# A transformer block on one Trainium2 core: a new written-out order for the first eight slots, and small moves in quad 3 and at the end

## The reference, cut to what matters

```python
q = (x @ Wk.T + bk);  k = (ctx @ Wk.T + bk);  v = (ctx @ Wv.T + bv)      # per head, q and k share Wk
scores = einsum(q, k) / sqrt(32)                                          # causal
p = softmax(where(allow, scores, -1e32))
dist = sqrt(clip((sum(p) - cumsum(p)) * abs(i - j), 0))
effect = clip(exp(-softplus(gamma) * dist), 1e-5, 1e5)
attn = softmax(where(allow, scores * effect, -1e32))
x1 = layer_norm(x + concat(attn @ v) @ Wo.T + bo)
out = layer_norm(x1 + relu(x1 @ W1.T + b1) @ W2.T + b2)                   # 2048 hidden features
```

## Time and profile before

| | |
|---|---|
| median of 3 runs | 1573.59 us (1573.33 to 1576.73) |
| the profiled execution | 1576.78 us, its span 1575.0 us |
| PE, PEld, DVE, ACT, POOL busy | 1476.0, 1232.7, 1165.7, 1037.4, 102.6 us |
| granted PE clock, mean | 0.972 |
| DMA | 334.13 MB, mean 212 GB/s |

### The profile page before, as it was taken

The page is one execution under the profiler, slowest core; times in us unless marked ns, Lnnn a source line. Parts: engine busy times, 40 slices in busy tenths (PEclk is TensorE's granted clock), DMA queues, the critical chain, the costliest instruction groups (busy, mean ns, idle before and its releaser), DMA issues.

```text
span 1575.0 us, 34730 instructions
## 1 busy us (share of the span) xinstructions
PE 1476.0 (94%) x13056; PEld 1232.7 (78%) x13056; DVE 1165.7 (74%) x3971; ACT 1037.4 (66%) x2679; POOL 102.6 (7%) x97
## 2 busy tenths in 40 slices
PE   4567899999999999999999999999999999999897
PEld 3455788878878887887888788788878878888786
DVE  5787769687787968778696877869687786968533
ACT  2776766766667676666767666676766667676622
POOL 4000101000010100001010000101000010100000
PEclk8777999999999999999999999999999999999999
DMA  5774556555665655565555556656555665654776
GB/s 214 245 250 186 191 186 213 206 197 201 213 221 197 220 202 194 203 213 219 198 221 204 191 203 218 220 191 226 201 189 207 216 222 190 223 201 176 269 290 255
DMA packets 62790, 334.13 MB, mean 212 GB/s; under 512 B 8224, under 2 KB 8224, under 8 KB 29472
## 3 DMA queue, kind: packets, MB, share of 16 engines
q1 hardware_dynamic: 62624, 331.92, 58.6%
HBM read 306.72 MB, written 25.17 MB: 211 GB/s over the span
## 4 chain that ended last, share of the span: by engine, by line
PE 64%; DVE 26%; ACT 7%; issue 1%; DMA 1%; POOL 1%; SPq 0%; POOLq 0%; DVEq 0%; ACTq 0%
PE bank L205 18%; PE bank L207 16%; PE bank L206 16%; PE bank L401 7%; DVE w_sb L1028 6%; DVE w_sb L1016 5%; PE bank L415 4%; DVE gz L1024 2%; DVE w_sb L1038 2%; DVE s_sb L1004 1%; ACT w_sb L698 1%; ACT w_sb L700 1%; PE bank L437 1%; ACT w_sb L696 1%; DVE rows L1098 1%
## 5 line engine op out<-in xcount | busy, mean ns | idle before, releaser
L205 PE MATMUL bank<-xt_hi,w_ring 128*128 128x256 f32 x1024 | 296.0, 289 | 0.9 <-ACT h_sb L777 0.9
L207 PE MATMUL bank<-xt_hi,w_ring 128*128 128x256 f32 x1024 | 287.7, 281 | 0.0
L206 PE MATMUL bank<-xt_lo,w_ring 128*128 128x256 f32 x1024 | 287.2, 281 | 0.0
L719 ACT COPY pt_sb<-bank 128x512 f32<-128x512 f32 x192 | 111.8, 582 | 203.7 <-PE bank L415 203.6
L1004 DVE CUSTOM_DVE_ANT_0 s_sb<-bank,mask 128x256 f32<-128x256 f32 (+7 forms) x512 | 129.9, 303 | 155.4 <-PE bank L401 154.4
L205 PE MATMUL bank<-w_ring,h_hi 128*128 128x512 f32 x512 | 211.3, 413 | 7.9 <-DVE h_lo L1111 6.4
L689 ACT ACTIVATE w_sb<-s_sb,nm 128x161 f32<-128x161 f32 (+7 forms) x512 | 164.1, 404 | 77.7 <-DVE nm L1012 77.7
L709 ACT ACTIVATE p_sb<-w_sb,nm 128x32 f32<-128x32 f32 (+7 forms) x512 | 205.7, 405 | 0.0
L207 PE MATMUL bank<-w_ring,h_lo 128*128 128x512 f32 x512 | 203.9, 398 | 0.0
L206 PE MATMUL bank<-w_ring,h_hi 128*128 128x512 f32 x512 | 202.5, 396 | 0.0
L401 PE MATMUL bank<-qk_sb 32*32 32x256 f32 (+7 forms) x4096 | 170.5, 294 | 33.6 <-DVE m L1004 27.1
(11 more groups left out here) (130 smaller groups left out, 2989.5 us busy)
## 6 DMA issues: line engine op xcount, KB each, us to landing
w_ring<-w_split SPq DMA_DIRECT2D x256, 1024.0 KB, 4.8
w_split<-w_ring SPq DMA_DIRECT2D x32, 512.0 KB, 5.1
x_raw<-x_t SPq DMA_DIRECT2D x16, 512.0 KB, 3.9
c_raw<-ctx_t SPq DMA_DIRECT2D x16, 512.0 KB, 5.0
u_sb<-x_rows SPq DMA_DIRECT2D x16, 512.0 KB, 5.9
ring_raw<-w SPq DMA_DIRECT2D x32, 256.0 KB, 5.6
out<-rows SPq DMA_DIRECT2D x15, 512.0 KB, 6.9
wk_raw<-wk SPq DMA_DIRECT2D x1, 1024.0 KB, 4.8
```

The lines of the kernel that those rows point to most:

```text
L205: nc.tensor.matmul(dst, a_hi, b_hi, start=start, stop=False)
L206: nc.tensor.matmul(dst, a_hi, b_lo, start=False, stop=False)
L207: return nc.tensor.matmul(dst, a_lo, b_hi, start=False, stop=stop)
L719: nc.scalar.copy(pt_sb[:, n], pt_bank[:]).then_inc(pt_ok, 1)
```

## The change

- The first eight slots have an order of their own (`first`) on every engine, in place of `step(0)` and `step(1)`. In it DVE masks all three groups of a slot before `decayed_scores` of the slot before; the splits are spread 0, 3, 3, 2, 2, 4, 2, 0 over slots 0 to 7; the rows' stage of batch 0 is written out in slot (1, 2).
- The cast of each `w1`/`w2` piece moves from ACT to POOL. The pieces are split in the order 4 to 15, 0 to 3, and 0 to 3 stay in the ring: the first two pairs of batch 0 are not read back.
- `wk` is loaded, cast and subtracted in two parts: the 128 columns of quad 0 first, the rest after. `gammas` are loaded by ACT's queue with a semaphore of their own (`gam_in`), as is `bk` (`bk_in`). POOL makes its constants in another order, and DVE, ACT and PE wait for the part each needs (`MASKS`, `STARTS`, `DISTS`, `CONSTS`); the 16 column memsets are four with strides. `l1b_bc` and `add_bias(0)` move to slot 4 on POOL. `values(0, *)` and `values(1, *)` go to the y banks, in slots (0, 1), (1, 0), (1, 1).
- In `step`, quad 3, the masks of groups 0 and 1 come before `rows_low(i-1, 0)` and `concat_low(i, 0)`.
- At the end `hidden_low(14, 1)` moves from `final` to the end of `step(15)`; both `project_rows(15, *)` follow each other into two banks; `turn_rows(15, *)`, `hidden(15, 0)` are each moved ahead of an `add_hidden` of batch 14.

In the diff, calls that follow each other are put on one line.

```diff
-            for i in range(B):
-                step(i, True, 1 <= i, 2 <= i, 3 <= i, i + 1 < B)
+            first()
+            for i in range(2, B):
+                step(i, True, True, True, 3 <= i, i + 1 < B)
...
+        SPLIT = [*range(4, FT), *range(4)]
+        SPLIT_BY = (0, 3, 6, 8, 10, 14, 16, 16)
...                                                  # SP, per slot n of the first eight
+                    for at in split_in(n):
+                        store_hidden(at)
+                        if 1 <= at and at + 3 < FT:
+                            raw_hidden(at + 3)
...                                                  # PE, slots 0, 1 and 6
+                scores(0, 0, 0); scores(0, 0, 1); scores(0, 0, 2)
+                pe.wait_ge(qk_ok, 1)
+                pe.wait_ge(wk_lo_ok, 2)
+                queries_keys(0, 1)
+                scores(0, 1, 0); scores(0, 1, 1); scores(0, 1, 2)
+                pe.wait_ge(qk_ok, 2)
+                queries_keys(0, 2)
+                values(0, 0, y_bank[0])
+                values(0, 1, y_bank[1])
...
+                scores(1, 2, 0); scores(1, 2, 1)
+                transposes(1, 0, 0)
+                scores(1, 2, 2)
+                project_rows(0, 0)
+                project_rows(0, 1, y_bank[1])
+                transposes(1, 0, 1)
+                pe.wait_ge(u_ok, 1)
+                queries_keys(1, 3)
...                                                  # PE, end
                 project_rows(last, 0)
+                pe.wait_ge(pt_ok, 12 * B)
+                project_rows(last, 1, pt_bank)
+                add_hidden(ffn, 5)
+                hidden(ffn, 7)
                 pe.wait_ge(u_ok, RT * last + 1)
-                add_hidden(ffn, 5)
-                project_rows(last, 1)
-                hidden(ffn, 7)
-                add_hidden(ffn, 6)
-                pe.wait_ge(u_ok, RT * last + 2)
                 turn_rows(last, 0)
                 turn_rows(last, 1)
+                add_hidden(ffn, 6)
+                hidden(last, 0)
                 add_hidden(ffn, 7)
-                hidden(last, 0)
                 hidden(last, 1)
...                                                  # DVE, slots 2, 3 and 6
+                totals(0, 0); masks(0, 2); decayed_scores(0, 1)
+                running_sums(0, 2); splits(2)
+                totals(0, 1); masks(0, 3); concat(0, 0); decayed_scores(0, 2)
+                inputs_low(1); concat_low(0, 0); running_sums(0, 3); splits(3)
...
+                totals(1, 0); masks(1, 2); splits(5)
+                residual(0, 0); residual(0, 1, y_bank[1])
+                moments1(0); weigh1(0); shift1(0)
+                decayed_scores(1, 1); rows_low(0, 0); rows_low(0, 1)
+                running_sums(1, 2); splits(6)
...                                                  # DVE, step, quad 3
                     totals(i, 1)
-                if last:
-                    rows_low(i - 1, 0)
-                if now:
-                    concat_low(i, 0)
                     mask_scores(i, 3, 0)
                     mask_scores(i, 3, 1)
+                if last:
+                    rows_low(i - 1, 0)
+                if now:
+                    concat_low(i, 0)
...                                                  # POOL
+            def split_high(at):
+                n = SPLIT[at] % 4
+                pool.wait_ge(raw_in[n], 32 * (at // 4 + 1))
+                nc.gpsimd.tensor_copy(w_ring[:, n::4, 0], ring_raw[:, n::4, 1]).then_inc(ffw_hi_ok, 1)
```

More of the change, by code:

```diff
@@ L337, in step @@
                             w2_behind(i - 1, 0)
[L338 to L347, removed]
             def final():
                 step(B, False, True, True, True, False)
-            over_batches(step, final)
+            over_batches(first, step, final)
             rows_out(B - 2)
@@ L1136, in finish_rows, with splits, masks, first @@
                                                    ALU.mult, ALU.add).then_inc(out_ok, 1)
+            def splits(n):
+                for at in split_in(n):
+                    split_low(at)
+            def masks(i, c):
+                for g in range(NS):
+                    mask_scores(i, c, g)
+            def first():
+                masks(0, 0)
+                key_weight_low(1, slice(P, D))
+                dve.wait_ge(const_ok, DISTS)
+                running_sums(0, 0)
+                splits(0)
+                masks(0, 1)
+                weight_low(1, wv_lo, wv_hi, wv_raw)
+                decayed_scores(0, 0)
+                running_sums(0, 1)
+                splits(1)
+                totals(0, 0)
+                masks(0, 2)
+                decayed_scores(0, 1)
+                running_sums(0, 2)
+                splits(2)
+                totals(0, 1)
+                masks(0, 3)
+                concat(0, 0)
+                decayed_scores(0, 2)
+                inputs_low(1)
+                concat_low(0, 0)
+                running_sums(0, 3)
+                splits(3)
+                totals(0, 2)
+                masks(1, 0)
+                concat(0, 1)
+                decayed_scores(0, 3)
+                concat_low(0, 1)
+                weight_low(2, wo_lo, wo_hi, wo_raw)
+                running_sums(1, 0)
+                splits(4)
+                totals(0, 3)
+                masks(1, 1)
+                concat(0, 2)
+                decayed_scores(1, 0)
+                concat_low(0, 2)
+                running_sums(1, 1)
+                concat(0, 3)
+                concat_low(0, 3)
+                totals(1, 0)
+                masks(1, 2)
+                splits(5)
+                residual(0, 0)
+                residual(0, 1, y_bank[1])
+                moments1(0)
+                weigh1(0)
+                shift1(0)
+                decayed_scores(1, 1)
+                rows_low(0, 0)
+                rows_low(0, 1)
+                running_sums(1, 2)
+                splits(6)
+                totals(1, 1)
+                mask_scores(1, 3, 0)
+                mask_scores(1, 3, 1)
+                inputs_low(2)
+                hidden_low(0, 0)
+                concat(1, 0)
+                mask_scores(1, 3, 2)
+                decayed_scores(1, 2)
+                concat_low(1, 0)
+                running_sums(1, 3)
+                concat(1, 1)
+                concat_low(1, 1)
@@ L1343, in add_bias, with first @@
                                         ALU.add).then_inc(xb_ok, 1)
+            def first():
+                for at in range(4):
+                    split_high(at)
+                for n in range(2 * NQ):
+                    if n == 2:
+                        inputs_high(1)
+                    for at in split_in(n):
+                        if 1 <= at and at + 3 < FT:
+                            split_high(at + 3)
+                    if n == 4:
+                        pool.wait_ge(s_mm, NS * (NQ + 1))
+                        pool.wait_ge(cons_in, 16 * 6)
+                        pool.wait_ge(const_ok, CONSTS + 1)
+                        nc.gpsimd.tensor_tensor(l1b_bc[:], l1b_bc[:], b2_bc, ALU.add).then_inc(col_ok, 1)
+                        add_bias(0)
+                    if n == 6:
+                        inputs_high(2)
+                    if n == 7:
+                        add_bias(1)
             def step(i, now, last, ffn, done, ahead):
-                if i == 0:
-                    add_bias(0)
                 if ahead:
@@ L1354, in final @@
                 pass
-            over_batches(step, final)
-CONSTS = 4 + 6 + 1 + 16 + 1 + 12 + 1 + 1 + 1
-COLS = 8
+            over_batches(first, step, final)
+MASKS = 8 + 4
+STARTS = MASKS + 4
+DISTS = STARTS + 4 + 1
+CONSTS = DISTS + 8 + 1 + 1
+COLS = 3
 def kernel(**inputs):
```

344 lines of the change are left out of this document (252 added, 92 removed).

## The result

The kernel after takes 1564.68 us (median of 6 runs, 1564.31 to 1568.86), the kernel before 1575.10 in the same session (6 runs, 1573.33 to 1576.73): ratio 0.9937, interval 0.9927 to 0.9948. It gains 10.4 us where 21.7 were forecast. The sign is right and the time lies in the range, but the likeliest case had its own range of 1546 to 1558, and the time is outside it. The profiled execution (1566.3 us, span 1564.5) is 10.5 us shorter in span than that of before.

The account below looks back on a forecast made before the run. PE was taken to bound from batch 2 on, DVE's sum the first eight slots; 16.4 + 0.3 + 5.0 = 21.7 us off the 1573.59 us median gave 1552 us, range 1536 to 1565, likeliest case (0.50) 1546 to 1558.

Parts of the forecast that it names:

- The first eight slots: Start to first scores of batch 2: these come at 170.8 us against 187.21, a gain of 16.4 us.
- DVE's work and POOL's effect on it: First eight slots: DVE busy 130.5 us, plus 9 us lost beside 16 casts on POOL, 0.56 us each.
- Standing still: First eight slots: DVE idle 3 us filling the pipe, 6 at slot (1, 2), 6 for slips of PE.
- The stall at piece 13: Slot (1, 2): DVE waits about 5.5 us for a late load and cast; 6 taken together with project_rows.
- The slips at the low clock: First eight slots: PE at mean clock 0.77 costs DVE 3 us, and 3 more in slot (1, 3).
- The masks of quad 3: Batches 2 to 14: PE's wait for the masks goes but returns for h_lo; gain 0.3 us, bounds 0 and 15.8.
- The end: After the last batches: shorter wait for h_lo, no low clock, covered waits; gain 5.0 us, bounds 2 and 6.5.
- the masks pay in full: Rival, quad 3: DVE's run to h_lo also starts earlier, all 15.8 us gained, 1536 us; chance 0.12.
- POOL and DVE at the worst: Rival, first eight slots: each cast on POOL costs DVE 1.45 us, 23 and not 9, 1566 us; chance 0.14.
- the cast's whole length: First eight slots, reading of the skill's port rule: each cast costs DVE its full 1.05 us, some 17 us.
- The casts did not become the chain: Rival, first eight slots: DVE waits for every POOL cast, slower than before, 1585 us; chance 0.04.
- PE at the low clock: Rival, first eight slots: PE at clock 0.50 bounds them, scores of batch 2 at 181 us, 1562 us; chance 0.05.

Follow-up runs that it names:

- experiment 3: Changed kernel with the w1/w2 casts back on ACT, 1559.78 us (e3_casts_on_act); also, separately, with the splits spread otherwise, 1561.96 us (e4_spread).
- experiment 1: Kernel before with only the quad 3 masks moved: 1578.31 us; changed kernel with that move taken back: 1562.52 us (e5_quad3_undone).
- experiment 4: Four traces with quad 3 masks moved or not compared for DVE's scans; then one run with an earlier u_sb load, 1574.26 us (e10_u_load_early).
- experiment 5: Changed kernel with the end of the kernel before: 1569.05 us; changed kernel with one end load asked for earlier: 1563.51 us (e6_end_loads).
- e6_end_loads: Changed kernel with SP asking for w1 pair 2 of batch 15 ahead of w2_behind(14, 7): 1563.51 us, ratio 0.9925.
- experiment 2: Changed kernel with hidden_low(i-1, 0) brought forward, 1542.31 us; then also with the quad 3 masks back in their old place, 1558.02 us (e9_early_quad3_undone).
- e9_early_quad3_undone: Changed kernel with hidden_low(i-1, 0) early and the quad 3 masks back in their old place: 1558.02 us, ratio 0.9887.
- e3_casts_on_act: Changed kernel with the casts of the w1 and w2 pieces back on ACT, at the ends of its slots: 1559.78 us, ratio 0.9899.
- e4_spread: Changed kernel with the splits spread 0, 3, 3, 3, 2, 3, 2 over the slots: 1561.96 us, ratio 0.9912.
- e5_quad3_undone: Changed kernel with the quad 3 masks back behind rows_low and concat_low: 1562.52 us, ratio 0.9919.
- e10_u_load_early: Changed kernel with SP asking for u_sb ahead of the last w2 pair instead of behind it: 1574.26 us, ratio 0.9996.

## Why the prediction was wrong

The first and third term had their mechanism right for the most part, and their size wrong; the second had its sign wrong. All three fell short.

**The first eight slots, forecast 16.4, measured 10.3.** This holds over half of the miss. 16.3 + 130.5 + 3 + 6 + 9 + 6 = 170.8 became 17.12 + 141.94 + 17.88 = 176.94.
- *Start*: first masks at 17.12 us, forecast 16.3; the gamma chain began at 12.14, as said. 0.8 us short.
- *DVE's work and POOL's effect on it*, 130.5 + 9 = 139.5 forecast, 141.94 measured. The casts' 9 us were right (9.2 by experiment 3, whose window ends on the same event). The other 2.4 us fit work of POOL that I had not costed and that experiment 3 leaves in place (132.77 for 130.5). `l1b` and the first bias addition moved into slot (1, 0), where DVE's eight products take 5.41 us and not 2.32, 3.1 us more. The second addition, at 166.24 us, holds `nm`, the negated maxima of 8 columns, for 2.29 us and not 0.17. Against this, one slot's small sums and one `h_lo`, some 2 us, now lie behind the first scores of batch 2. The two rows of DVE in after:

```profile
116.52 5.41 DVE L1229 SCALAR_TENSOR_TENSOR w_sb<-w_sb,gz,dist 128x160 f32<-128x160 f32 x8
...
166.37 2.29 DVE L1244 TENSOR_SCALAR nm<-m 128x8 f32<-128x8 f32 x1
```

- *Standing still*, 3 + 6 + 6 = 15 forecast, 17.88 measured. The stall at piece 13 was 5.3 us for "about 5.5". Filling the pipe, 3 us forecast, took 1.8 (1.1 for ACT's exponentials, 0.7 for the masks of (0, 1)). The slips at the low clock were put at 6 us in sum by a glance at PE's load. What occurred in their place is 6.2 us of waiting for score group 2 between two masks, of which 5 x 0.76 = 3.8 are the low clock; that the sizes agree is luck. The chain would have let me work it out: group 2 cannot start before the masks of group 0 have read its bank. What I had left out are `cc_lo`'s waits for ACT, 2.4 us, and the 2.2 us of short gaps.

The failed step is this addition of DVE's sum and its covers: "so DVE is the bound of the stage, and its sum is what counts". I listed what stands still from the engines' loads, slot by slot, and did not walk one slot's order through PE, DVE and POOL. I also added up DVE to the first scores of batch 2, though the chain leaves it 17.8 us earlier, at 159.12. The longer `cc_lo` wait (1.8 us at 174.9) and the held `nm` at 166.37 lie in this last part, beside the chain, and so did not delay the scores. How the forecast's sum would have come out up to 159.12 alone, it does not say, so the 6.1 us cannot be shared out to the last: 0.8 are the start, 3.1 the products at 116.52, 0.6 the other `cc_lo` wait, and the rest stays open.

**The masks of quad 3, forecast 0.3, measured -2.7** (-2.1 and -2.2 by the medians of experiment 1)**.** That the wait only moves to `h_lo` was right to 0.3 us in 18 (18.5 for the 18.2 that 1.4 x 13 makes), and the sign of the rest was wrong. The step that failed is the lower bound of 0: the edit shifts PE against POOL, and POOL's addition already held DVE in every batch (`gz` 1.92 us in each, 36.0 us in all). The race that it now wins in five batches makes 2.2 of the 2.7 us (experiment 4).

**The end, forecast 5.0, measured 3.0** (2.7 and 3.9 in experiment 5), and 4.4 to 4.8 in the three traces whose clock does not drop. The first wait shrank as said, 4.10 to 1.48 us, and so did the low clock. The load of pair 2 was late by 1.78 us where I had taken 1.1, but the stretch at a lower clock behind it, 1.7 us in after's trace, was not in the sum. `e6_end_loads` has wait and clock back, 3.5 us by its trace.

Of the rivals, "the masks pay in full" fell as it stood, and came true when `h_lo` was computed earlier, close to the condition named for it (15.7 us for 15.8): experiment 2 starts DVE's run no earlier, but takes `h_lo` ahead of the eight products in it. POOL and DVE at the worst, 1.45 us a cast, fell at 0.57, and so did the cast's whole length, 17 us in sum. The casts did not become the chain, but for the one of piece 13. PE at the low clock was not the bound: it stood idle for 7.19 us ahead of group 2 at 49.05.

## What to carry to other kernels

A wait removed is worth only what the next meeting of the same two engines lets through: find it, and move both, since one alone paid -2.2 and 4.5 us here and both together 20.2. Where a stage is bound by one engine's sum, the idle time in it comes from short hand-overs, so follow one slot's order through all engines before adding up, and end the sum where the chain leaves the engine. An operation on POOL that has ample time is not free; its length is paid by DVE, and which run of DVE it falls into decides whether PE pays as well.

## What the runs showed of the hardware

- The same addition on POOL (128x1024, 2.4 us) held a scan by 2.2 us (2.57 to 4.78), or a `gz` of 8 columns by 1.7 (0.23 to 1.92), or an `nm` of 8 columns by 2.1 (0.17 to 2.29), or one of a run of small two-input maxima. `gz` and `nm` are TENSOR_SCALAR operations that write 8 columns. In these traces the one that began later was slowed: POOL took 2.41 us ahead of the scan at 257.76, and 3.64 where it began 1.1 us behind a scan (at 269.08 in before).
- The wait of 1.78 us for a load at 1516 us was followed by a granted clock of 0.57 over 4 us, one of 2.09 us in `e9_early_quad3_undone` by 0.50 (1512 to 1514 us). Those of 1.69 to 1.84 us for the same load in `e3_casts_on_act`, `e4_spread` and `e5_quad3_undone` were not (1.00), nor those of 2.2 us in the batches of `e10_u_load_early` (1.00 over all of 190 to 1430 us). The length of the one pause alone does not say whether the clock falls; what else does was not tried.
